# Jumping knowledge layers of a graph kernel: four blocks become one, with messages turned before they are weighed

## The chip, the core and the metric

The kernel runs on one core of a Trainium2 chip, as one launch. The metric is the device time of that launch in microseconds. Engines are called by the profile's names: PE is TensorE, DVE VectorE, ACT ScalarE, POOL GpSimd, SP SyncE. Each has its own stream of instructions, and they meet only through semaphores.

## What is computed

Four graph networks run one after the other over 50000 nodes of 128 features and 25000 edges (src, dst), sorted by dst; each adds its result to its input and normalizes the rows. The change is in the third, a stack of four layers whose outputs are combined by a maximum ("jumping knowledge"):

```python
norm_src = rsqrt(max(deg_out, 1))[:, None]
norm_dst = rsqrt(max(deg_in, 1))[:, None]
h = x
xs = []
for i in range(4):
    m = h * norm_src
    agg = segment_sum(m[src], dst, num_segments=n)
    h = agg * norm_dst
    h = relu(h @ Ws[i] + bs[i])
    mu, var = mean(h, axis=0), var(h, axis=0)          # over all nodes
    h = (h - mu) * rsqrt(var + 1e-5) * gammas[i] + betas[i]
    h = relu(h)
    xs.append(h)
out = relu(max(stack(xs), axis=0) @ lin1_w + lin1_b)
```

## The kernel before

The kernel works on edges in **slots**: 49 groups (`EG`) of 512 slots (`GROUP`), four columns (`SUB`) of 128. The sum of a node's messages stands in the slot of its last edge. Nodes without an edge all have the same row in these layers; it stands once, in row `SLOTS` of a table.

The program is a chain of blocks. A block has one stream for each engine and ends with a barrier of all of them. `run_groups(eng, n, stages)` writes an engine's stream as a software pipeline: in step k it emits, in the order of the list, each stage for group k minus its lag. Order within an engine is therefore fixed: an instruction that waits holds up all behind it. `g.lag(2)` is the group two earlier, whose buffer is used again.

`jk_start_block` makes the edge weights `l2_weight` (one number a slot, slots along the partitions) and the rows `SLOTS` of the tables `jk0` to `jk2`. Then `jk_layer_block` runs once for each layer i. For each group:

- POOL (`pool_fetch`, L570) issues four indirect DMAs that gather 128 rows each of the last layer's table into one of five message buffers. It waits until the buffer is used up.
- In layers 1 to 3 DVE (`adjust`, L1908, L1910) applies the last layer's batch norm to the rows: times a row of scales, plus a row of shifts. These rows were made at the last layer's end by `spread_column` and two products with ones on PE.
- ACT (`scalar_weigh`, L1023) scales each of the four columns by its edge weight, with the ReLU.
- PE (`tensor_sum`, L1057) transposes the four columns, so that slots lie along the free dimension.
- DVE (`vector_carry`, L1079) scans along the slots: running sums that start again with each node.
- PE (`make`, L696) multiplies by the layer's weights; ACT (`keep`, L1886) adds the bias, with ReLU.
- SP stores this tile `h_t` into `jk_t` (for the maximum at the end). Except in the last layer, PE turns it back (`turn`, L687), ACT copies the rows out of PSUM (`out`, L1891), and SP stores them into `jk{i}`, from which the next layer gathers.
- DVE (`count`, L1916, L1919) adds up values and squares for the batch norm, over last slots only.

After group 48, DVE and ACT compute mean, variance, scale and shift (L1926 to L1938), and the rows are spread. Only then does the block end, and POOL begins the next layer's gathers.

Of the kernel before, what the change touches and what calls it, by code (L numbers as in the profile page):

```python
# [299 lines left out]
class Weights:  # L300
    def __init__(self, nc, ctx):
# [15 lines left out]
        self.jk_scale_row, self.jk_shift_row = sb("jk_scale_row", [P, D]), sb("jk_shift_row", [P, D])  # L317
# [1459 lines left out]
def spread_column(dve, pe_ready, diag, ident, column):  # L1777

    dve.tensor_scalar(diag[:], ident[:], column, None, ALU.mult).then_inc(pe_ready, 1)


def jk_start_block(nc, K, W, tables):


    ph = Phase(nc, "jk_start", 0)
    row, row_ps = ph.sb("row", [LAYERS, D]), ph.ps("row_ps", [LAYERS, D])
    made, turned, copied, stored = (ph.sem(n) for n in ("made", "turned", "copied", "stored"))
    chain, to_root, root = ph.sem("chain"), ph.sem("to_root"), ph.sem("root")
    block = ph.block()

    @block.scalar
    def _(act):
        act.wait_ge(to_root, 1)
        act.activation(K.l2_weight[:], K.l2_weight[:], ACT.Sqrt).then_inc(root, 1)

    @block.vector
    def _(dve):
        link = linker(dve, chain)
        dve.tensor_scalar(K.l2_weight[:], K.src_count[:], 1.0, None, ALU.max).then_inc(to_root, 1)
        dve.tensor_scalar(W.jk_const[:], W.jk_b[:], 0.0, None, ALU.max).then_inc(made, 1)  # L1800
# [12 lines left out]
    def _(sp):
        sp.wait_ge(copied, 1)
        for i in range(LAYERS - 1):
            sp.dma_start(tables[f"jk{i}"][SLOTS:SLOTS + 1], row[i:i + 1, :]).then_inc(stored, 16)
        sp.wait_ge(stored, 16 * (LAYERS - 1))
    ph.close()


def jk_layer_block(nc, i, K, W, tables):


    ph = Phase(nc, f"jk_layer{i}", EG)
    S, A_ = ph.count_sem, ph.dma_sems
    last = i == LAYERS - 1
    sums = SegmentSums(ph, K, tables["x2"] if i == 0 else tables[f"jk{i - 1}"], K.idx if i == 0 else K.idx_jk, D, [K.l2_weight])
    h_t, h = ph.sb("h_t", [P, 2, 1, GROUP]), ph.sb("h", [P, 2, SUB, D])
    off, square = ph.sb("off", [P, GROUP]), ph.sb("square", [P, GROUP])
    off_sum, square_sum = ph.sb("off_sum", [P, EG]), ph.sb("square_sum", [P, EG])  # L1830
    small, diag = ph.sb("small", [P, 4]), [ph.sb(f"diag{b}", [P, P]) for b in range(2)]
    h_ps, rows_ps = ([ph.ps(f"{k}{b}", [P, 1, GROUP]) for b in range(2)] for k in ("h_ps", "rows_ps"))
    made, kept, turned, out_done, offset, counted = (S(n) for n in ("made", "kept", "turned", "out_done", "offset", "counted"))
    scaled, shifted = (S(n) for n in ("scaled", "shifted"))
    if i:
        ready = ph.sb("ready", [P, 2, SUB, D])
        sums.rows, sums.messages, sums.used, sums.func = ready, shifted, scaled, ACT.Relu
# [5 lines left out]
    def _(sp):  # L1843
# [9 lines left out]
        if not last:  # L1853
            wait_for_all(sp, h_stored)
# [710 lines left out]
```

## Time and profile before

| what | us |
|---|---|
| median of three runs | 6712.33 |
| lowest and highest run | 6707.89, 6729.76 |
| span of the profiled execution | 7555.6 |
| the profiled execution's own time, beside its span | not recorded |
| the blocks of the change, 4000 to 5295 us of the span | 1295.00 |

The profiled execution is one execution under the hardware profiler, and it is longer than every timed run; its span is from its first to its last instruction. Times of single instructions come from it. The end of a matmul is modelled by the profiler and not recorded, and some matmul records can be missing. What the profile names as the releaser of a wait is inferred from semaphores; semaphores are used again by later blocks, so that a name such as `sage_nodes_x_in` can stand for a semaphore that by then counts something else.

### The profile page before, as it was taken

To read this page: it belongs to the slowest core of one execution; us is meant where nothing else is said; L and a number is where in the kernel's file an instruction comes from. 1 tells how busy PE (TensorE), PEld (TensorE's weight loads), DVE (VectorE), ACT (ScalarE), POOL (GpSimd) and SP (SyncE) were. 2 spreads that over 40 slices of the span, in tenths; PEclk is the share of its full clock that TensorE was granted. 3 is DMA by queue.
4 is the path that set the end of the run, shared out by engine and by line. 5 is a ranking of instruction groups with operands and counts; after the bars stand their busy time and mean duration, and the time that the engine had idled before them with its cause. 6 is when DMAs were issued, how large, how long until landed. Compare 5 with 4: busy or idle time off the path is not lost. (4 is left out here: it accounts for less than half of the span.)

```text
span 7555.6 us, 86623 instructions
## 1 busy us (share of the span) xinstructions
PE 4855.1 (64%) x23532; PEld 3254.8 (43%) x23532; DVE 4654.8 (62%) x13695; ACT 3050.2 (40%) x6979; POOL 3999.0 (53%) x3991
## 2 busy tenths in 40 slices
PE   6888888779978625686233443434899995579211
PEld 4666665445558403575222222211555553346111
DVE  4777666223358627668674455656899995644444
ACT  3555554443334103344343333333677773245000
POOL 4565553544435466556555565656333334654766
PEclk9999999889989755796555666766899997789555
DMA  6988665776768423696343475754677675565232
GB/s 143 226 240 231 209 206 188 215 215 226 243 201 245 121 45 92 187 257 185 109 122 103 124 118 110 128 96 88 234 248 256 244 251 156 173 183 177 84 88 73
DMA packets 1104141, 1292.14 MB, mean 171 GB/s; under 512 B 133903, under 2 KB 815679, under 8 KB 1097390
## 3 DMA queue, kind: packets, MB, share of 16 engines
q1 hardware_dynamic: 973518, 1032.63, 43.5%
q0 software_dynamic: 130144, 253.97, 16.5%
q8 instruction: 197, 3.23, 0.2%
q14 instruction: 282, 2.31, 0.1%
HBM read 607.93 MB, written 682.10 MB: 171 GB/s over the span
## 5 line engine op out<-in xcount | busy, mean ns | idle before, releaser
L570 POOL DMA_INDIRECT jk_layer_msg<-jk,idx_jk x588 | 593.7, 1010 | 376.5 <-issue 173.4
L1057 PE MATMUL jk_layer_sum_ps<-ident,jk_layer_weighted 128*128 128x128 f32 x784 | 178.9, 369 | 733.6 <-ACT jk_layer_weighted L1023 382.1
L2084 POOL TENSOR_TENSOR rows_moved<-rows_x_in,w_lonely_row 128x512 f32<-128x512 f32 x98 | 124.6, 1272 | 677.3 <-DVE rows_x L671 640.9
L1057 PEld LDWEIGHTS jk_layer_sum_ps<-ident,jk_layer_weighted 128*128 128x128 f32 x784 | 114.6, 183 | 844.8 <-ACT jk_layer_weighted L1023 431.5
L1079 DVE TENSOR_TENSOR_SCAN jk_layer_sum_t<-goes_on,jk_layer_sum_t,jk_layer_sum_ps 128x512 f32<-128x512 uint8 x196 | 250.1, 1276 | 346.3 <-DMA sage_nodes_x_in<-in_x 288.0
L1886 ACT ACTIVATE jk_layer_h_t<-jk_layer_h_ps,w_jk_b 128x512 f32<-128x512 f32 x196 | 134.7, 687 | 631.8 <-DMA gat_own<-yv 337.9
L696 PE MATMUL sage_nodes_h_ps<-sage_nodes_h_t,w_ws 128*128 128x512 f32 x784 | 353.6, 594 | 0.0
L1198 DVE COPY sage_h<-sage_turn 128x512 f32<-128x512 f32 x98 | 67.8, 692 | 456.7 <-PE sage_turn L687 348.3
L894 ACT ACTIVATE sage_nodes_h_t<-sage_nodes_h_ps,w_b_c 128x512 f32<-128x512 f32 x392 | 248.9, 688 | 239.8 <-PE sage_nodes_h_ps L696 114.8
L696 PE MATMUL sage_h_ps<-sage_sum_t,w_wn 128*128 128x512 f32 x588 | 296.7, 614 | 59.0 <-issue 58.8
L2283 PE MATMUL gcn_end_sum_ps<-ident,gcn_end_rows 128*128 128x128 f32 x196 | 54.7, 434 | 426.9 <-DVE gcn_end_rows L2276 215.4
L570 POOL DMA_INDIRECT sage_msg<-h,idx x196 | 185.7, 948 | 247.4 <-ACT sage_weighted L1023 166.4
L570 POOL DMA_INDIRECT sage_end_msg<-h,idx x196 | 193.8, 989 | 224.4 <-ACT sage_end_weighted L1023 113.5
L696 PE MATMUL jk_layer_h_ps<-jk_layer_sum_t,w_jk_w 128*128 128x512 f32 x392 | 297.0, 852 | 0.6 <-DVE jk_layer_sum_t L1079 0.4
L687 PE MATMUL sage_nodes_ring<-ident,sage_nodes_h_t 128*128 128x128 f32 x1568 | 221.9, 288 | 106.7 <-issue 98.7
L696 PE MATMUL sage_h_ps<-sage_own_t,w_ws 128*128 128x512 f32 x588 | 290.0, 602 | 0.0
L1627 POOL DMA_INDIRECT second_msg<-u,idx_y x196 | 185.4, 946 | 182.4 <-PE second_x_ps L679 108.3
L1137 POOL DMA_INDIRECT place_of_src<-place,src_node x196 | 185.5, 947 | 167.7 <-issue 67.6
L1179 ACT ACTIVATE sage_h_t<-sage_h_ps,w_b_c 128x512 f32<-128x512 f32 x196 | 124.3, 685 | 357.9 <-PE sage_h_ps L696 296.6
L570 POOL DMA_INDIRECT jk_layer_msg<-x,idx x196 | 194.4, 992 | 139.2 <-issue 57.7
L570 POOL DMA_INDIRECT gcn_msg<-r,idx x196 | 191.9, 979 | 142.4 <-DVE gcn_rows L2276 65.8
L557 POOL DMA_INDIRECT src_count<-counts,src_node x196 | 192.3, 981 | 138.3 <-SPq L135 93.6
(454 smaller groups left out, 16299.8 us busy)
## 6 DMA issues: line engine op xcount, KB each, us to landing
h<-sage_nodes_h SPq DMA_DIRECT2D x196, 512.0 KB
h_t<-sage_h_t SPq DMA_DIRECT2D x98, 512.0 KB
h<-sage_h SPq DMA_DIRECT2D x98, 512.0 KB
jk_t<-jk_layer_h_t SPq DMA_DIRECT2D x196, 256.0 KB
rows_layers<-jk_t SPq DMA_DIRECT2D x49, 1024.0 KB, 5.9
r<-rows_h SPq DMA_DIRECT2D x98, 512.0 KB
second_x_in<-u SPq DMA_DIRECT2D x147, 260.0 KB
jk<-jk_layer_h SPq DMA_DIRECT2D x147, 256.0 KB
```

Of the source, the lines that this page charges most:

```text
L557: pool.indirect_dma_start(out=self.K.src_count[:, t:t + 1], out_offset=None, in_=self.table, in_offset=bass.IndirectOffsetOnAxis(ap=self.K ...
L570: pool.indirect_dma_start(out=into[:, g.number % depth, s, :], out_offset=None, in_=table, in_offset=bass.IndirectOffsetOnAxis(ap=index_ti ...
L687: mm = pe.transpose(ps[:, n, c * P:(c + 1) * P], feats[:, c, s * P:(s + 1) * P], ident[:])
L696: mm = pe.matmul(ps[:, c, :], w[:, k, c * P:(c + 1) * P], x[:, k, :], start=n == 0, stop=n == len(terms) - 1)
L894: ins = act.activation(tile[:, g.b, c, :], ps[:, c, :], ACT.Relu, bias=bias[:, c:c + 1])
L1057: mm = pe.transpose(ps[:, c, at_s], self.weighted[:, g.b, s, c * P:(c + 1) * P], self.K.ident[:])
L1079: dve.tensor_tensor_scan(self.sum_t[:, g.b, c, :], self.K.goes_on[:, cols(g, GROUP)], self.ps[g.b][:, c, :], self.sum_t[:, 1 - g.b, c, GRO ...
L1137: pool.indirect_dma_start(out=K.place[:, t:t + 1], out_offset=None, in_=tables["place"], in_offset=bass.IndirectOffsetOnAxis(ap=K.src_node ...
L1179: ins = act.activation(h_t[:, g.b, c, :], h_ps[:, c, :], ACT.Relu, bias=bias[:, c:c + 1])
L1627: pool.indirect_dma_start(out=msg[:, r % 4, s, :], out_offset=None, in_=tables["u"], in_offset=bass.IndirectOffsetOnAxis(ap=K.idx_y[:, col ...
L1886: act.activation(h_t[:, g.b, 0, :], h_ps[g.b][:, 0, :], ACT.Relu, bias=W.jk_b[:, i:i + 1]).then_inc(kept.sem, 1)
L2084: pool.tensor_tensor(moved[:, g.b], x_in[:, g.number % 3], to_subs(W.lonely_row), ALU.add).then_inc(lonely_added.sem, 1)
```

## The change

`jk_start_block` and the four `jk_layer_block` become one `jk_block`. Groups are counted on through all layers (`job(i, g)`), with one barrier at the end. In detail:

- POOL's message ring is 8 deep; its first gather of layer i waits only for the last three stores of the rows of layer i-1, and no longer for that layer's statistics.
- PE transposes the raw messages (`turn_messages`). In layers 1 to 3 ACT then applies the last batch norm and ReLU on the transposed tile (`norm`), where scale and shift are one number a partition. The rows of scales and shifts and their spreading go.
- The edge weights are turned once, stored in DRAM as `l2_row`, and for each group of each layer SP loads the 512 weights into all 128 partitions (`load_weight`). DVE multiplies (`weigh`), out of PSUM in layer 0, out of SBUF in the others. ACT's four scalings go.
- The scan's input is now a tile in SBUF, `product`. `sum_t`, `h_t` and `h` have three buffers instead of two.
- PE's stages are `turn_messages` at lag 0, `make` at 2 and `turn` at 3, where they were 0, 1 and 2.

```diff
-    sums = SegmentSums(ph, K, tables["x2"] if i == 0 else tables[f"jk{i - 1}"], ..., D, [K.l2_weight])
+    deep = 8
+    msg = ph.sb("msg", [P, deep, SUB, D])
+    weight = ph.sb("weight", [P, 3, GROUP])
...
     @block.sync
+        sp.wait_ge(l2_copied, 1)
+        sp.dma_start(tables["l2_row"].rearrange("(h q p) -> q h p", h=2, p=P), l2_rows[:]).then_inc(l2_stored, 16)
+        sp.wait_ge(l2_stored, 16)
+        for i in layers:
+            def load_weight(g):
+                j = job(i, g)
+                wait_for(sp, weighed, j.lag(3))
+                sp.dma_start(weight[:, j.number % 3, :], tables["l2_row"][cols(g, GROUP)].partition_broadcast(P)).then_inc(weight_in.of(j), 16)
...
+            run_groups(sp, EG, [(load_weight, -2), (store_t, 2)] + ([] if i == LAST else [(store, 3)]))
     @block.gpsimd
+            if i:
+                for k in range(3):
+                    wait_for(pool, h_stored, Group(i * EG - 1 - k))
...
     @block.tensor
+            def turn_messages(g):
+                j = job(i, g)
+                wait_for(pe, arrived, j)
...
+                turn_rows(pe, msg_ps[j.b][:, 0, :], msg[:, j.number % deep], K.ident).then_inc(msg_turned.sem, 1)
...
+            run_groups(pe, EG, [(turn_messages, 0), (make, 2)] + ([] if i == LAST else [(turn, 3)]))
     @block.scalar
+            def norm(g):
+                j = job(i, g)
+                wait_for(act, msg_turned, j)
+                wait_for(act, weighed, j.lag(2))
+                act.activation(ready[:, j.b], msg_ps[j.b][:, 0, :], ACT.Relu, bias=W.jk_shift[:, i - 1:i], scale=W.jk_scale[:, i - 1:i]).then_inc(normed.sem, 1)
...
+            run_groups(act, EG, ([(norm, 0)] if i else []) + [(keep, 2)] + ([] if i == LAST else [(out, 3)]))
     @block.vector
-            dve.tensor_tensor(m, sums.msg[:, g.number % sums.depth], to_subs(W.jk_scale_row), ALU.mult).then_inc(scaled.sem, 1)
-            dve.tensor_tensor(m, m, to_subs(W.jk_shift_row), ALU.add).then_inc(shifted.sem, 1)
+                dve.tensor_tensor(product[:, j.b], rows, weight[:, j.number % 3], ALU.mult).then_inc(weighed.sem, 1)
...
+                dve.tensor_tensor_scan(sum_t[:, j.number % 3, 0, :], K.goes_on[:, cols(g, GROUP)], product[:, j.b], ...)
+            run_groups(dve, EG, [(carry, 1), (weigh, 0), (count, 3)])
```

On ACT, the border between layer 0 and layer 1 stood as follows; `jk_layer_small` is the column of statistics, the two L135/L1878 rows are the block's end and the next one's beginning:

```order
L1886 ACTIVATE jk_layer_h_t<-jk_layer_h_ps,w_jk_b 128x512
L1891 COPY jk_layer_h<-jk_layer_rows_ps 128x512 x2
L1897 ACTIVATE jk_layer_small<-jk_layer_small,w_eps 128x1
L135 UNCONDITIONAL_BRANCH
L1878 UNCONDITIONAL_BRANCH
L1023 ACTIVATE jk_layer_weighted<-jk_layer_ready,l_weight 128x128 x8
L1886 ACTIVATE jk_layer_h_t<-jk_layer_h_ps,w_jk_b 128x512
L1023 ACTIVATE jk_layer_weighted<-jk_layer_ready,l_weight 128x128 x4
L1886 ACTIVATE jk_layer_h_t<-jk_layer_h_ps,w_jk_b 128x512
```

Now the same place reads as follows (`jk_ready` is the tile after the batch norm):

```order
L1905 ACTIVATE jk_h_t<-jk_h_ps,w_jk_b 128x512
L1911 COPY jk_h<-jk_rows_ps 128x512 x2
L1916 ACTIVATE jk_small<-jk_small,w_eps 128x1
L1896 ACTIVATE jk_ready<-jk_msg_ps,w_jk_shift,w_jk_scale 128x512 x3
L1905 ACTIVATE jk_h_t<-jk_h_ps,w_jk_b 128x512
L1896 ACTIVATE jk_ready<-jk_msg_ps,w_jk_shift,w_jk_scale 128x512
L1905 ACTIVATE jk_h_t<-jk_h_ps,w_jk_b 128x512
L1911 COPY jk_h<-jk_rows_ps 128x512
L1896 ACTIVATE jk_ready<-jk_msg_ps,w_jk_shift,w_jk_scale 128x512
L1905 ACTIVATE jk_h_t<-jk_h_ps,w_jk_b 128x512
L1911 COPY jk_h<-jk_rows_ps 128x512
```

The block's end has gone, and three norms of layer 1 come before its first `keep`, where eight scalings did.

On DVE, one group in the middle of layer 1 was `count`, `adjust` and the scan:

```order
L1910 TENSOR_TENSOR jk_layer_ready<-jk_layer_ready,w_jk_shift_row 128x512
L1079 SCALAR_TENSOR_TENSOR jk_layer_sum_t<-goes_on,jk_layer_sum_t,jk_layer_sum_ps 128x512
L1916 SCALAR_TENSOR_TENSOR jk_layer_off,jk_layer_off_sum<-jk_layer_h_t,w_jk_const,last_row 128x512
L1919 SCALAR_TENSOR_TENSOR jk_layer_square,jk_layer_square_sum<-jk_layer_off 128x512
L1908 TENSOR_TENSOR jk_layer_ready<-jk_layer_msg,w_jk_scale_row 128x512
```

Now it is one product in place of the two operations of `adjust`, with its input from ACT and the weights from SP:

```order
L1963 SCALAR_TENSOR_TENSOR jk_square,jk_square_sum<-jk_off 128x512
L1952 SCALAR_TENSOR_TENSOR jk_sum_t<-goes_on,jk_sum_t,jk_product 128x512
L1941 TENSOR_TENSOR jk_product<-jk_ready,jk_weight 128x512
L1960 SCALAR_TENSOR_TENSOR jk_off,jk_off_sum<-jk_h_t,w_jk_const,last_row 128x512
L1963 SCALAR_TENSOR_TENSOR jk_square,jk_square_sum<-jk_off 128x512
```

On SP, the start of layer 0 had only the tables' rows and stores:

```order
L1816 DMA jk<-jk_start_row 1x128 x3
L135 UNCONDITIONAL_BRANCH
L1842 UNCONDITIONAL_BRANCH
L1846 DMA jk_t<-jk_layer_h_t 128x512 x2
L1850 DMA jk<-jk_layer_h 128x4x128
L1846 DMA jk_t<-jk_layer_h_t 128x512
L1850 DMA jk<-jk_layer_h 128x4x128
L1846 DMA jk_t<-jk_layer_h_t 128x512
```

Now the weights' row is stored first, and each step begins with a load:

```order
L1817 DMA jk<-jk_const_row 1x128 x3
L1819 DMA l_row<-jk_l_rows 98x2x128
L1825 DMA jk_weight<-l_row 128x512 x5
L1830 DMA jk_t<-jk_h_t 128x512
L1825 DMA jk_weight<-l_row 128x512
L1830 DMA jk_t<-jk_h_t 128x512
L1835 DMA jk<-jk_h 128x4x128
L1825 DMA jk_weight<-l_row 128x512
L1830 DMA jk_t<-jk_h_t 128x512
L1835 DMA jk<-jk_h 128x4x128
L1825 DMA jk_weight<-l_row 128x512
```

The loads of weights stand ahead of the stores in SP's queue, five of them before the first store.

## Rows read from the trace of the kernel before

**Rows 1.** Head of the page.

```profile
span 7555.6 us, 86623 instructions
```

**Rows 2.** Windows of layers 0 to 3: their sum; us busy by engine.

```profile
sum 1295.00, PE 537.90 PEld 299.71 DVE 725.62 ACT 441.89 POOL 788.10; mean PE 134.47 PEld 74.93 DVE 181.40 ACT 110.47 POOL 197.03
```

**Rows 3.** Groups by line, POOL, layer 0, then layer 1: busy, mean ns | idle, releasers.

```profile
L570 POOL DMA_INDIRECT jk_layer_msg<-x,idx x196 | 194.4, 992 | 139.2 <-issue 57.7 <-POOLq L137 40.9 <-ACT jk_layer_weighted L1023 40.5
...
L570 POOL DMA_INDIRECT jk_layer_msg<-jk,idx_jk x196 | 197.5, 1007 | 129.1 <-issue 57.3 <-DVE jk_layer_ready L1908 42.6 <-POOLq L137 29.1
```

**Rows 4.** Timeline, end of layer 0: start, us, engine, line, names [idle before].

```profile
4302.04 1.11 PE L1057 MATMUL jk_layer_sum_ps<-ident,jk_layer_weighted 128*128 128x128 f32 x4 [3.44 <-ACT jk_layer_weighted L1023]
...
4302.95 1.91 PE L696 MATMUL jk_layer_h_ps<-jk_layer_sum_t,w_jk_w 128*128 128x512 f32 x2
...
4304.90 0.69 ACT L1886 ACTIVATE jk_layer_h_t<-jk_layer_h_ps,w_jk_b 128x512 f32<-128x512 f32 x1 [2.44 <-PE jk_layer_h_ps L696]
...
4309.66 0.69 ACT L1886 ACTIVATE jk_layer_h_t<-jk_layer_h_ps,w_jk_b 128x512 f32<-128x512 f32 x1 [2.45 <-PE jk_layer_h_ps L696]
...
4313.12 0.69 ACT L1886 ACTIVATE jk_layer_h_t<-jk_layer_h_ps,w_jk_b 128x512 f32<-128x512 f32 x1 [1.14 <-PE jk_layer_h_ps L696]
```

**Rows 5.** Timeline, layer 0, near its start.

```profile
4028.35 0.66 PE L1057 MATMUL jk_layer_sum_ps<-ident,jk_layer_weighted 128*128 128x128 f32 x4 [1.44 <-issue]
...
4035.99 1.28 DVE L1079 TENSOR_TENSOR_SCAN jk_layer_sum_t<-goes_on,jk_layer_sum_t,jk_layer_sum_ps 128x512 f32<-128x512 uint8 x1 [7.66 <-DMA sage_nodes_x_in<-in_x]
...
4040.19 0.69 ACT L1886 ACTIVATE jk_layer_h_t<-jk_layer_h_ps,w_jk_b 128x512 f32<-128x512 f32 x1 [11.43 <-DMA gat_own<-yv]
```

**Rows 6.** Waits in the block of last rows: in total, times, longest.

```profile
ACT rows_y L2171 <- PE rows_bank_y L705: 7.8, 11, 0.7
```

**Rows 7.** Groups by line, POOL, the whole kernel.

```profile
L570 POOL DMA_INDIRECT jk_layer_msg<-jk,idx_jk x588 | 593.7, 1010 | 376.5 <-issue 173.4 <-DVE jk_layer_ready L1908 114.5 <-POOLq L137 88.6
...
L1627 POOL DMA_INDIRECT second_msg<-u,idx_y x196 | 185.4, 946 | 182.4 <-PE second_x_ps L679 108.3 <-issue 46.3 <-POOLq L137 24.7
```

**Rows 8.** Groups by line and shape, layer 1.

```profile
L1079 DVE TENSOR_TENSOR_SCAN jk_layer_sum_t<-goes_on,jk_layer_sum_t,jk_layer_sum_ps 128x512 f32<-128x512 uint8 x49 | 62.5, 1275 | 80.9 <-DMA sage_nodes_x_in<-in_x 70.9 <-DMA gat_own<-yv 10.0
L1023 ACT ACTIVATE jk_layer_weighted<-jk_layer_ready,l_weight 128x128 f32<-128x128 f32 x196 | 62.2, 389 | 22.4 <-DVE jk_layer_ready L1910 14.7 <-issue 7.7
...
L1916 DVE SCALAR_TENSOR_TENSOR jk_layer_off<-jk_layer_h_t,w_jk_const,last_row 128x512 f32<-128x512 f32 x49 | 36.4, 744 | 25.1 <-ACT jk_layer_h_t L1886 13.0 <-issue 12.1
...
L1908 DVE TENSOR_TENSOR jk_layer_ready<-jk_layer_msg,w_jk_scale_row 128x512 f32<-128x512 f32 x49 | 33.6, 686 | 17.2 <-DMA jk_layer_msg<-jk,idx_jk 17.1
```

**Rows 9.** Timeline: start of layer 0, then the border to layer 1.

```profile
4001.19 0.26 DVE L1799 TENSOR_SCALAR l_weight<-src_count 128x196 f32<-128x196 f32 x1 [3.45 <-PEq L137]
...
4005.52 0.95 POOL L570 DMA_INDIRECT jk_layer_msg<-x,idx  x1 [40.89 <-POOLq L137]
...
4009.27 0.95 POOL L570 DMA_INDIRECT jk_layer_msg<-x,idx  x1 [0.31 <-issue]
...
4011.74 1.28 ACT L1023 ACTIVATE jk_layer_weighted<-jk_layer_msg,l_weight 128x128 f32<-128x128 f32 x4 [9.89 <-DMA jk_layer_msg<-x,idx]
...
4297.27 0.95 POOL L570 DMA_INDIRECT jk_layer_msg<-x,idx  x1 [0.30 <-issue]
...
4320.47 0.20 DVE L1926 TENSOR_REDUCE jk_layer_small<-jk_layer_off_sum 128x1 f32<-128x49 f32 x1
...
4327.35 0.95 POOL L570 DMA_INDIRECT jk_layer_msg<-jk,idx_jk  x1 [29.12 <-POOLq L137]
```

**Rows 10.** DMA queues in 280 us of layer 1, then 270 us of layer 3.

```profile
q0 software_dynamic: 5810, 11.91, 47.3%
q1 hardware_dynamic: 26901, 21.18, 22.6%
...
q0 software_dynamic: 5820, 11.94, 38.3%
q1 hardware_dynamic: 5765, 10.50, 10.3%
```

More of the change, by code:

```diff
@@ L1791, in _, with keep, out @@
     @block.scalar
     def _(act):
-        act.wait_ge(to_root, 1)
-        act.activation(K.l2_weight[:], K.l2_weight[:], ACT.Sqrt).then_inc(root, 1)
+        act.wait_ge(l2_capped, 1)
+        act.activation(K.l2_weight[:], K.l2_weight[:], ACT.Sqrt).then_inc(l2_root, 1)
+        for i in layers:
+            def norm(g):
+                j = job(i, g)
+                wait_for(act, msg_turned, j)
+                wait_for(act, weighed, j.lag(2))
+                act.activation(ready[:, j.b], msg_ps[j.b][:, 0, :], ACT.Relu, bias=W.jk_shift[:, i - 1:i], scale=W.jk_scale[:, i - 1:i]).then_inc(normed.sem, 1)
+            def keep(g):
+                j = job(i, g)
+                wait_for(act, made, j)
+                wait_for(act, ht_stored, j.lag(3))
+                wait_for(act, counted, j.lag(3))
+                if i < LAST:
+                    wait_for(act, turned, j.lag(3))
+                act.activation(h_t[:, j.number % 3, 0, :], h_ps[j.b][:, 0, :], ACT.Relu, bias=W.jk_b[:, i:i + 1]).then_inc(kept.sem, 1)
+            def out(g):
+                j = job(i, g)
+                wait_for(act, turned, j)
+                wait_for(act, h_stored, j.lag(3))
+                act.copy(h[:, j.number % 3], lanes(rows_ps[j.b][:, 0, :], D)).then_inc(out_done.sem, 1)
+            if i:
+                act.wait_ge(scale_ready, i)
+            run_groups(act, EG, ([(norm, 0)] if i else []) + [(keep, 2)] + ([] if i == LAST else [(out, 3)]))
+            act.wait_ge(to_root, i + 1)
+            act.activation(small[:, 3:4], small[:, 1:2], ACT.Sqrt, bias=W.eps[:]).then_inc(rooted, 1)
@@ new lines, in _ @@
+        dve.tensor_scalar(K.l2_weight[:], K.src_count[:], 1.0, None, ALU.max).then_inc(l2_capped, 1)
+        dve.tensor_scalar(W.jk_const[:], W.jk_b[:], 0.0, None, ALU.max).then_inc(const_made, 1)
+        dve.wait_ge(const_turned, 1)
+        dve.tensor_copy(const_row[:], const_ps[:]).then_inc(const_copied, 1)
+        dve.wait_ge(l2_root, 1)
+        link(dve.reciprocal(K.l2_weight[:], K.l2_weight[:]))
+        dve.tensor_tensor(K.l2_weight[:], K.l2_weight[:], K.norm_dst[:], ALU.mult).then_inc(l2_ready, 1)
@@ L2528, in resnorm_gnn @@
         mean_block(nc, A, K, W, tables)
-        jk_start_block(nc, K, W, tables)
-        for i in range(LAYERS):
-            jk_layer_block(nc, i, K, W, tables)
+        jk_block(nc, K, W, tables)
         ends.close()
```

259 lines of the change are left out of this document (126 added, 133 removed).

## The prediction

> **What bounds the kernel now.** I read the page first [rows 1]: the profiled execution spans 7555.6 us, and it is 843 us longer than the median of the three timed runs, 6712.33 us (span over median 1.126). No other time of that execution is given. So whatever the trace shows must be read with the question which part of it the profiled execution alone has. The windows by stage come second: the five blocks that the change touches, from 4000 to 5295 us, take 1295 us of the span in four nearly equal layers [rows 2].
>
> Third, the groups by line on POOL. In each layer POOL issues 196 gathers; one takes 0.99 to 1.01 us and is followed by 0.30 us of issue [rows 3]. Four gathers make a group: 49 x 4 x 1.29 = 252 us a layer, 1008 of the 1295 us. The rest of layers 0 and 1 on POOL is a wait for ScalarE or VectorE to free one of the five message buffers (40.5 and 42.6 us) and the wait at the border between blocks (40.9 and 29.1 us).
>
> Why does POOL ever wait for a buffer? The timeline says that the engines behind it can go faster: with the slow TensorE clock (a product of 1.91 us) ScalarE's `keep` comes after 4.76 us, with the fast one after 3.46 us [rows 4], against 5.15 us for four gathers. But now and then TensorE's results come late. Its four transposes are shown to end at 4029.01, yet the scan that needs them starts at 4035.99, with VectorE idle for 7.66 us, and `keep` waits 11.43 us, to 4040.19 [rows 5]; nothing that VectorE or ScalarE wait for there is a DMA, whatever the inferred releaser says. These delays return with about every fifth group. In the block of last rows, where no gather runs, nothing like it exists: the longest wait of ScalarE for TensorE's `bank_y` is 0.7 us [rows 6].
>
> So the main question is whether the timed runs have these delays. POOL's waits for another engine in just three of its sixteen groups of indirect DMAs, 114.5 and 40.5 us here and 108.3 in the block `second`, are already 263 us [rows 3, 7], and such waits are the only large idle that could go away between profiled and timed execution, since one gather needs its 1.25 us either way. I take it as likelier that most of the 843 us are these delays, and that the timed kernel is bound by POOL in these layers: 4 x 252 + borders, some 1075 us.
>
> **The change, part by part.** *Weighing.* ScalarE loses four scalings of 389 ns a group and, in layers 1 to 3, gains one norm of a 128x512 tile out of PSUM, like `keep`'s 0.69 us: 1.56 becomes 0.69 us. VectorE loses the multiply by the row of scales and the add of the row of shifts (686 ns, and the add alike) and gains one product of the same size; in layer 0 it only gains the product [rows 4, 8]. PE's work is the same: four transposes, one product, four turns. All of it lies beside POOL's 5.15 us a group, so it is worth nothing there; without POOL as cover it would be the 4.76 us step that shrinks, at most by 0.7 us x 196 = 137 us.
>
> *Eight buffers instead of five, three instead of two behind.* Worth what POOL waits for buffers: nothing if the timed runs have no delays, 40.5 + 114.5 = 155 us if they have all of them [rows 3, 7].
>
> *Borders.* Before, the last gather of layer 0 starts at 4297.27 and the first of layer 1 at 4327.35; of this, 6.88 us are statistics, spreading of the rows and the barrier, from 4320.47 [rows 9]. Without late results I build the same border from rows: 2.47 us from the last gather's start to the scaling that needs it (4009.27 to 4011.74), scaling 1.28, on PE sum, product, turn, product 1.11 + 1.91 + 1.06 (four transposes, like the sum) + 1.91 [rows 4], `keep` 0.69, `count` 1.7 (two passes like the 744 ns one [rows 8] with their small reads), then 6.88: 19.0 us. After, POOL no longer waits for statistics, only for the stored rows: 2.47, but PE now has three products and four turns left behind the last transposes, 1.1 + 5.7 + 4.2 = 11.0, copy 0.57, store about 2.5 (as a gather): 16.6 us. With the fast clock, PE parts nearly halved, it is 16.2 against 11.7. Between 2.4 and 4.5 us, so 3.4 x 3 = 10 us gained. The start: POOL's first gather is at 4005.52 and could follow the barrier at about 4001.7, as VectorE does at 4001.19 [rows 9]: 4 us gained. The row of weights must be turned, stored and loaded first, two DMA trips of 2.5 us behind 4004; the first product is then ready near 4010, about when the first messages are.
>
> *Port between VectorE and POOL.* A gather takes 946 ns on average in the block `second`, 992 in layer 0 and 1007 in layer 1 [rows 3, 7]. What goes up with it is VectorE's work with two SBUF inputs: two operations of about 0.7 us in layer 0, four in layer 1 [rows 8]. If a gather that meets one waits for its end, the cost grows with the sum of squared lengths: 0.5 gives 46 ns, 1.0 gives 61 ns. After, the scan (1275 ns) has its data in SBUF and no longer in PSUM. If it counts like the others the sum is 1.3 to 1.6, some 85 to 95 ns: 35 ns x 784 = 27 us lost. If it doesn't count, layers 1 to 3 have three operations instead of four: 8 us gained. I take 10 us lost. The Trainium skill (SBUF — State Buffer, "Who interferes with whom") says that a VectorE instruction with two SBUF inputs contends with a GpSimd instruction that reads SBUF; by that the scan counts and the loss would be the 27 us. The same section infers that a tensor_tensor doesn't touch descriptor writing; the rise from 946 to 1007 ns doesn't bear that out.
>
> *DMA.* 196 loads of 256 KB are new. In 280 us of layer 1, 11.91 MB of gathers (45.4 groups) took 47.3% of the sixteen engines and 21.18 MB of stores 22.6%: 2.92 + 1.57 = 4.5 us a group. In layer 3, with half the stores, gathers took 2.27 us a group and the stores 10.3% of 270 us for 10.50 MB, 2.65 us a MB [rows 10]. A load is 0.26 MB, 0.7 us a group: 5.2 us in layers 1 and 2, as much as POOL's 5.15; 3.6 to 4.1 in the others. I take nothing for it, with 8 buffers as cover; the dear end is under the rivals.
>
> The sum: -10 - 4 + 10 + 0 = -4 us, to 6708 us.
>
> **The rivals.** *The delays are real.* For it: the trace has them, and the other 843 us may be in DMAs or issue. Against it: that POOL's idle would then leave no room for the 843 us. Then 155 us of POOL's buffer waits go, and 14 us at borders: 6543 us. Eight buffers hold 41 us of gathers, more than the longest delay here. If half is real: 6630 us.
>
> *DMA becomes the bound in layers 1 and 2* (the other side). For it: gathers there cost 0.65 us a group more than in layer 3, where one 256 KB stream less runs beside them; another stream may cost as much again. Then 5.2 + 0.65 = 5.85 us a group, 0.7 over POOL: 49 x 2 x 0.7 = 69 us lost; with 0.3 it is 34. It decides from the point where the DMA engines need over 5.15 us a group. Against it: part of a packet's time is waiting and not work. With the scan at the port (27 us) and 14 us gained at borders this gives 6712 + 34 to 69 + 13 = 6760 to 6795 us.
>
> *The scan alone takes the port:* 6712 - 14 + 27 = 6725 us, still no change that can be told.
>
> **How the numbers follow.** About 0.3%, 20 us, is what a measurement of this kernel can tell. Forecast (6692 to 6732 us, the port case within it): 0.33. Delays real, wholly 0.2 or partly 0.2: faster, 0.40. DMA bound, or DMA and port: slower, 0.27. The predicted time is the single likeliest case's, 6708. The range goes from 6540, which leaves out little under the full gain, to 6770, which takes in the lower price of the DMA case; both bounds of port and borders lie inside. Likeliest case alone: 6690 to 6735.
>
> **What would show it.** POOL's gaps for buffers gone in the changed trace, with a time that stays, would show that the timed runs never had them; a time 100 us or more lower, that they had. Mean of a gather near 1.03 us: the scan takes the port; near 0.99: it doesn't. Packets of layers 1 and 2 at over 0.9 share of the DMA engines, and POOL, TensorE waiting for messages: DMA bound. The border between layers should fall from 30 us to 12 to 17. I am wrong above all if one gather is cheaper in timed runs than 1.25 us, since then the engines behind POOL set the pace and what they lose in work counts.

## The result and the profile after

| | us, median (lowest to highest) | runs |
|---|---|---|
| before | 6718.84 (6707.89 to 6729.76) | 4 |
| changed | 6787.66 (6778.96 to 6807.84) | 4 |

The ratio is 1.0108, 95% interval 1.0093 to 1.0123: 69 us slower. I had forecast 6708 us, no change.

The changed kernel's profiled execution lasted as long as its timed runs, 6786.5 us, so its trace can be read as it stands. The trace behind the prediction could not be, so I profiled the kernel before once more (first experiment below, 6721.6 us); the comparison here is with that. First the groups of gathers on POOL, of the changed kernel (layers 1 to 3, then layer 0), which answer to [rows 3, 7]:

```profile
L1853 POOL DMA_INDIRECT jk_msg<-jk,idx_jk x588 | 628.7, 1069 | 276.1 <-issue 174.6 <-DMA jk<-jk_h 90.8 <-PE jk_msg_ps L679 10.6
L1853 POOL DMA_INDIRECT jk_msg<-x,idx x196 | 217.5, 1110 | 80.2 <-issue 57.3 <-POOLq L137 20.8 <-PE jk_msg_ps L679 2.1
```

and the same of the kernel before, profiled again:

```profile
L570 POOL DMA_INDIRECT jk_layer_msg<-jk,idx_jk x588 | 593.3, 1009 | 257.9 <-issue 174.6 <-POOLq L137 71.1 <-DVE jk_layer_ready L1908 12.2
...
L570 POOL DMA_INDIRECT jk_layer_msg<-x,idx x196 | 196.3, 1002 | 85.2 <-issue 59.4 <-POOLq L137 25.8
```

A gather went from 1009 to 1069 ns in layers 1 to 3 and from 1002 to 1110 ns in layer 0: 588 x 60 + 196 x 108 ns = 56 us more. Waits for buffers are small in both (10.6 and 2.1 us against 12.2). The wait for the last layer's rows or the barrier, 90.8 us for three borders, was 71.1 us.

Now one window for each layer with the border behind it; a row ends with the granted clock, the busy share of the DMA engines, and GB/s. The changed kernel:

```profile
core 0: us, PE busy (x) PEld busy (x) DVE busy (x) ACT busy (x) POOL busy (x), PEclk, DMA share, GB/s
3460.00:3745.00 285.00, 141.12 (x480) 88.64 (x481) 158.29 (x290) 56.76 (x94) 217.51 (x196) 0.72 0.62 175
3745.00:4045.00 300.00, 137.95 (x467) 81.02 (x466) 149.03 (x284) 91.83 (x140) 208.03 (x196) 0.67 0.92 166
4045.00:4350.00 305.00, 146.38 (x489) 86.78 (x486) 158.77 (x302) 95.89 (x147) 208.48 (x196) 0.70 0.90 166
4350.00:4660.00 310.00, 137.29 (x338) 61.56 (x336) 182.39 (x357) 81.25 (x116) 212.21 (x196) 0.63 0.68 138
```

and the kernel before, profiled again:

```profile
3465.00:3738.00 273.00, 148.09 (x487) 85.52 (x487) 135.88 (x250) 118.41 (x294) 196.34 (x196) 0.70 0.54 140
3738.00:4023.00 285.00, 147.96 (x481) 87.20 (x482) 193.59 (x353) 117.10 (x292) 198.49 (x196) 0.68 0.87 133
4023.00:4311.00 288.00, 148.33 (x493) 85.65 (x491) 194.72 (x355) 118.09 (x294) 197.61 (x196) 0.69 0.87 134
4311.00:4597.00 286.00, 124.31 (x318) 54.84 (x318) 202.81 (x383) 98.61 (x254) 197.16 (x196) 0.67 0.55 96
```

In both kernels the DMA engines are busy 0.87 to 0.92 of the time in layers 1 and 2, and much less in layers 0 and 3 (0.54 to 0.68). The kernel before was thus at the edge already. In the first profile layer 1 read 47.3% and 22.6%, 0.70 together [rows 10]: its pace was slower, and a group's gathers took less of the DMA engines there (2.92 us, against 3.59 in run 1).

Last the border between layers 1 and 2 of the changed kernel, POOL's last gather of one layer and first of the next, with VectorE's scans between them:

```profile
4025.82 0.95 POOL L1853 DMA_INDIRECT jk_msg<-jk,idx_jk  x1 [0.31 <-issue]
4062.64 0.94 POOL L1853 DMA_INDIRECT jk_msg<-jk,idx_jk  x1 [35.87 <-DMA jk<-jk_h]
```

```profile
4036.18 1.28 DVE L1952 TENSOR_TENSOR_SCAN jk_sum_t<-goes_on,jk_sum_t,jk_product 128x512 f32<-128x512 uint8 x1
...
4039.36 1.28 DVE L1952 TENSOR_TENSOR_SCAN jk_sum_t<-goes_on,jk_sum_t,jk_product 128x512 f32<-128x512 uint8 x1
```

POOL has issued everything at 4027 and then waits 35.87 us. Ten scans follow each other at 3.18 us from 4026.62 to 4055.28: VectorE, no longer held up by anything, works off the groups that are left. What held it up before shows in the waits from 3912 to 4026 (in total, times, longest):

```profile
DVE jk_product L1941 <- DMA jk_weight<-l_row: 68.9, 13, 8.4
ACT jk_h L1911 <- DMA jk<-jk_h: 49.5, 13, 7.3
...
PE jk_msg_ps L679 <- DMA jk_msg<-jk,idx_jk: 8.6, 4, 3.7
```

VectorE waits for weights and ScalarE for the end of a store, so that its buffer can be used again. TensorE waits little for messages here and from 3952 on not at all; earlier in the layer it did (91.5 us from 3752 to 3912). So when the DMA engines fall behind, what is late at the end of a layer are the loads and stores on SP's queue. A ring of eight message buffers hides this from POOL, but the groups that are not worked off when the last gather is issued are paid for at the border. The same border of the kernel before, profiled again, was shorter:

```profile
4037.03 0.94 POOL L570 DMA_INDIRECT jk_layer_msg<-jk,idx_jk  x1 [28.18 <-POOLq L137]
```

From the first gather's start and the last one's end in each layer, on POOL's timeline, I made this ledger (us; "end" is from the last gather to the next block's first instruction):

| kernel | layers 0 / 1 / 2 / 3 | borders | end | in all |
|---|---|---|---|---|
| before, profiled again | 255.8 / 262.1 / 261.4 / 256.6 | 17.5 / 28.2 / 25.4 | 16.2 | 1123.2 |
| changed | 276.9 / 274.4 / 267.9 / 271.6 | 14.8 / 35.9 / 40.2 | 17.1 | 1198.8 |

The block is 75.6 us longer: 54.9 in the layers, 19.8 in the borders, 0.9 at the end. It starts 5 us earlier (the wait in front of its first gather is 20.8 us, was 25.8), which leaves 71 us of the 69 measured.

### The profile page after: what moved, and what is told of

Read it like the earlier page. It is cut to its first block and busy times, and to the rows that moved or that the text cites. A ratio compares the mean times of both kernels' runs of the same rounds, so it can differ in the third digit from the quotient of the medians.

```text
span 6786.5 us, 85990 instructions
## 1 busy us (share of the span) xinstructions
PE 4757.1 (70%) x23518; PEld 3216.2 (47%) x23522; DVE 4564.9 (67%) x13586; ACT 2932.8 (43%) x6342; POOL 4063.1 (60%) x3991
## 5 line engine op out<-in xcount | busy, mean ns | idle before, releaser
L1853 POOL DMA_INDIRECT jk_msg<-jk,idx_jk x588 | 628.7, 1069 | 276.1 <-issue 174.6
L679 PE MATMUL jk_msg_ps<-ident,jk_msg 128*128 128x128 f32 x784 | 187.3, 384 | 501.9 <-DMA jk_msg<-jk,idx_jk 360.5
L679 PEld LDWEIGHTS jk_msg_ps<-ident,jk_msg 128*128 128x128 f32 x784 | 127.9, 195 | 604.2 <-DMA jk_msg<-jk,idx_jk 452.2
L696 PE MATMUL jk_h_ps<-jk_sum_t,w_jk_w 128*128 128x512 f32 x392 | 319.6, 912 | 124.3 <-DVE jk_sum_t L1952 124.3
L1905 ACT ACTIVATE jk_h_t<-jk_h_ps,w_jk_b 128x512 f32<-128x512 f32 x196 | 134.7, 687 | 381.9 <-PE jk_h_ps L696 327.2
L1853 POOL DMA_INDIRECT jk_msg<-x,idx x196 | 217.5, 1110 | 80.2 <-issue 57.3
L599 POOL DMA_INDIRECT kept<-u,idx x196 | 194.9, 994 | 113.1 <-issue 59.4
L570 POOL DMA_INDIRECT sage_nodes_fetched<-in_x,src_x x196 | 205.4, 1048 | 95.1 <-issue 49.1
L671 DVE TENSOR_SCALAR rows_z<-rows_y,rows_norm_moments,rows_norm_root 128x128 f32<-128x128 f32 x392 | 255.5, 711 | 3.6
L570 POOL DMA_INDIRECT gcn_end_msg<-y,idx x196 | 188.6, 962 | 108.3 <-issue 59.4
```

The lines of the kernel that those rows point to most:

```text
L570: pool.indirect_dma_start(out=into[:, g.number % depth, s, :], out_offset=None, in_=table, in_offset=bass.IndirectOffsetOnAxis(ap=index_ti ...
L599: pool.indirect_dma_start(out=kept[:, t, :], out_offset=None, in_=table, in_offset=bass.IndirectOffsetOnAxis(ap=K.idx[:, t:t + 1], axis=0) ...
L671: ins = dve.tensor_scalar(out[:, g.number % depth, s, :], rows[:, g.b, s, :], self.moments[:, g.b, s, 0:1], self.root[:, g.b, s, 0:1], ALU ...
L679: mm = pe.transpose(ps[:, s * P:(s + 1) * P], rows[:, s, :], ident[:])
L696: mm = pe.matmul(ps[:, c, :], w[:, k, c * P:(c + 1) * P], x[:, k, :], start=n == 0, stop=n == len(terms) - 1)
L1853: pool.indirect_dma_start(out=msg[:, j.number % deep, s, :], out_offset=None, in_=table, in_offset=bass.IndirectOffsetOnAxis(ap=index[:, g ...
```

## The experiments

Two theories. **Port:** the scan's data now come from SBUF, a gather that meets the scan waits, and POOL's pace falls. **DMA:** the loads of weights overload the DMA engines, transfers come late, and borders pay. Ratios are to the kernel before on the same chip. Ledgers are made as the one above.

### 1. The kernel before, profiled again

No edit.

> The kernel before, profiled a second time. If the late TensorE results belonged only to the first profiled execution, the span is 6700 to 6740 us, ScalarE's longest wait for TensorE in the four layers is under 4 us, the layers take 1125 to 1140 us in all (1200 us of the changed kernel less the 70 us by which it is slower), and POOL waits for buffers under 15 us. If they are real, the span is over 7000 us and POOL's waits for buffers are again some 150 us.

It took 6723.41 us with a span of 6721.6. These are its waits of ScalarE's `keep` for TensorE, and of POOL for a buffer, in the four layers (in total, times, longest):

```profile
ACT jk_layer_h_t L1886 <- PE jk_layer_h_ps L696: 333.5, 161, 2.9
...
POOL jk_layer_msg L570 <- DVE jk_layer_ready L1908: 12.2, 12, 3.8
```

The longest is 2.9 us where the first profile had 11.43 [rows 5]; POOL's waits for buffers are 12.2 us where it had 155 [rows 3, 7]. This execution took as long as the timed runs (6707.89 to 6729.76 us), so the late TensorE results are not in them.

### 2. Weights loaded for three groups only

```diff
-                wait_for(sp, weighed, j.lag(3))
-                sp.dma_start(weight[:, j.number % 3, :], ...)
+                if j.number < 3:
+                    sp.dma_start(weight[:, j.number % 3, :], ...)
...
-                wait_for(dve, weight_in, j)
+                if j.number < 3:
+                    wait_for(dve, weight_in, j)
```

All later groups are weighed with the weights of the first three, so this kernel leaves out part of the computation.

> The changed kernel, but weights are loaded for the first three groups only and used for all groups (the other groups' weights are left out of the computation). Theory DMA (the 193 other loads make messages late, and the backlog of up to eight groups is paid at the borders): the borders between layers fall from 36 and 40 us to 12 to 17, a gather falls to about 1.0 us, and the time is 6700 to 6725 us. Theory port (the scan's SBUF input lengthens the gathers): a gather stays at 1.07 to 1.11 us and only the borders' part is gained, 6740 to 6760 us.

6745.57 us, ratio 1.0036 (1.0022 to 1.0050): 42 us of the loss are gone. Theory DMA alone had expected 6700 to 6725 us, theory port alone 6740 to 6760.

```profile
L1853 POOL DMA_INDIRECT jk_msg<-jk,idx_jk x588 | 631.0, 1073 | 226.2 <-issue 176.4 <-DMA jk<-jk_h 48.0 <-PE jk_msg_ps L679 1.8
```

The borders are 15.3 / 17.7 / 15.0 us, 43 less than in the changed kernel, and the gathers stayed long, at 1073 and, in layer 0, 1094 ns. So the loads cost at the borders and not through the gather's length. Each theory had half of it right: the borders fell as DMA said, the gathers stayed long as port said. There are two causes.

### 3. Product in PSUM

```diff
-                dve.tensor_tensor(product[:, j.b], rows, weight[:, j.number % 3], ALU.mult).then_inc(weighed.sem, 1)
+                dve.tensor_tensor(product[j.b][:], rows, weight[:, j.number % 3], ALU.mult).then_inc(weighed.sem, 1)
...
-                dve.tensor_tensor_scan(sum_t[:, j.number % 3, 0, :], K.goes_on[:, cols(g, GROUP)], product[:, j.b],
+                dve.tensor_tensor_scan(sum_t[:, j.number % 3, 0, :], K.goes_on[:, cols(g, GROUP)], product[j.b][:],
```

Here `product` is two PSUM tiles.

> The changed kernel with the product written to PSUM, so that the scan reads its data from PSUM as before. Theory port: the mean gather falls by 0.06 to 0.1 us to about 1.0 us, which is 784 x 0.075 = 59 us, 6725 to 6740 us. Theory DMA: no change, 6780 to 6795 us, gathers within 0.02 us of 1.07 and 1.11.

6768.21 us, 1.0076 (1.0059 to 1.0093). Layers 1 to 3, layer 0, then the window of layer 1:

```profile
L1854 POOL DMA_INDIRECT jk_msg<-jk,idx_jk x588 | 585.7, 996 | 310.0 <-issue 171.9 <-DMA jk<-jk_h 96.8 <-PE jk_msg_ps L679 41.4
...
L1854 POOL DMA_INDIRECT jk_msg<-x,idx x196 | 194.7, 993 | 80.2 <-issue 57.6 <-POOLq L137 20.8 <-PE jk_msg_ps L679 1.8
```

```profile
3740.00:4010.00 270.00, 117.48 (x395) 69.21 (x396) 122.61 (x223) 74.86 (x114) 194.08 (x196) 0.68 0.94 154
```

The mean gather falls to 996 and 993 ns, 66 us in all. The edit moves the product's write as well as the scan's input, but the timelines tell the two apart: 93 gathers start in the first 1.1 us of a scan here, and none takes over 0.95 us; in the changed kernel 104 of 106 such gathers took over 1 us. So the length is the scan's: shown. But only 20 us arrive in the time. POOL now waits 41.4 us for buffers and 96.8 us at the borders (16.2 / 46.6 / 33.9), and VectorE 208.5 us for weights where it had waited 154.0, with the DMA engines busy 0.94 of layer 1. What the port gives back, the DMA engines take. Neither theory had this number.

### 4. Five buffers instead of eight

```diff
-    deep = 8
+    deep = 5
```

> The changed kernel with five message buffers in place of eight. If messages are late because the DMA engines lack time, depth only shifts where it is paid: POOL waits for buffers, the borders fall to some 25 us, and the time stays within 10 us of 6788. If the depth itself does harm, since loads of weights stand behind eight groups of gathers in the DMA engines' rings, the time falls by 20 to 60 us, and VectorE's wait for weights (154 us) at least halves.

6783.21 us, 1.0095 (1.0078 to 1.0112), which can't be told from the changed kernel. The later borders are 24.5 and 29.5 us instead of 35.9 and 40.2, and the layers 8.2 us longer. VectorE waits 144 us for weights (154 in the changed kernel), so the depth isn't what delays them. Depth shifts the bill and hardly changes it.

### 5. The constant row 128 times

Of the 25000 edges, 16290 come from a node that has no incoming edge. All of these messages are read from one row, `SLOTS`, in layers 1 to 3. Here each partition has its own copy:

```diff
-        dve.tensor_scalar(K.idx_jk[:], where[:], float(SLOTS), None, ALU.min)
+        link(dve.tensor_copy(first_copy[:], K.slot_no[:, 0:1]))        # partition number
+        link(dve.tensor_scalar(first_copy[:], first_copy[:], float(SLOTS), None, ALU.add))
+        dve.tensor_scalar(K.idx_jk[:], where[:], first_copy[:], None, ALU.min)
...
-            sp.dma_start(tables[f"jk{i}"][SLOTS:SLOTS + 1], const_row[i:i + 1, :]).then_inc(const_stored, 16)
+            sp.dma_start(tables[f"jk{i}"][SLOTS:SLOTS + P], const_row[:, i, :]).then_inc(const_stored, 16)
```

> The changed kernel, but the constant row of the nodes without an edge stands 128 times at the end of each table, and each partition gathers its own copy. Theory hot row (the gathers' packets of layers 1 to 3 are slow because 65% of them read one and the same row): the mean packet of a gather falls from 0.6 to 0.85 us to layer 0's 0.28 us, the borders of layers 1 to 2 and 2 to 3 fall from 36 and 40 us to 15 to 18, the mean gather on POOL stays at 1.06 to 1.11 us, and the time is near that of the kernel with weights loaded once, 6735 to 6755 us. Rival (packets are slow because of the loads and stores beside them): borders and time stay, 6775 to 6795 us.

6750.62 us, 1.0040 (1.0025 to 1.0054). DMA queues in 260 us of layer 1 (packets, MB, share of 16 engines), changed kernel, then this one:

```profile
q0 software_dynamic: 5898, 12.09, 60.3%
q1 hardware_dynamic: 29750, 29.05, 34.5%
```

```profile
q1 hardware_dynamic: 35520, 34.61, 41.1%
q0 software_dynamic: 5837, 11.94, 20.0%
```

The same 12 MB of gathers take 20.0% instead of 60.3%, as in layer 0 of the changed kernel (20.4%); the borders are 15.9 / 15.0 / 14.4 us, and the gather on POOL stays long (1092 ns). All the loads of weights are still there. So at this kernel's pace it takes both, a hot row (one that most gathers read) and the loads, to make transfers late; taking away either gives back some 40 us.

### 6. Runs 2 and 3 together

The two edits above in one kernel.

> The changed kernel with both: weights loaded for the first three groups only (the others' weights are left out of the computation), and the product in PSUM. If port and DMA are the two causes and add up: gathers at 0.99 us, layers of 254 to 257 us, borders of 15 to 18 us, in all 1085 us from the first gather to the end of the block, 38 us under the kernel before: 6675 to 6700 us. If a third thing holds the layers, over 6710 us.

6717.05 us, 0.9993 (0.9982 to 1.0005), higher than the 6675 to 6700 expected. Gathers are 1011 and 991 ns, the layers 253.7 to 259.7, but the borders 12.7 / 32.1 / 22.4 us, where run 2 had 15.3 / 17.7 / 15.0 at the slower pace. At POOL's faster pace the hot row alone makes transfers late, as in the kernel before.

### 7. Weights spread by TensorE

```diff
+            def spread_weight(g):
+                wait_for(pe, weighed, j.lag(2))
+                for s in range(SUB):
+                    mm = pe.matmul(weight_ps[j.b][:, s * P:(s + 1) * P],
+                                   K.l2_weight[:, g.number * SUB + s:g.number * SUB + s + 1].broadcast_to([P, P]), K.ident[:], start=True, stop=True)
+                mm.then_inc(spread.sem, 1)
...
-                dve.tensor_tensor(product[:, j.b], rows, weight[:, j.number % 3], ALU.mult).then_inc(weighed.sem, 1)
+                dve.tensor_tensor(msg_ps[j.b][:, 0, :], rows, weight_ps[j.b][:], ALU.mult).then_inc(weighed.sem, 1)
```

`rows` is ScalarE's tile in layer 0 too; the scan reads `msg_ps`; the loads of weights go.

> The changed kernel, but TensorE spreads the weights: four products of a column of weights (the same for all output partitions) with the identity write 128x512 weights to PSUM; ScalarE copies the messages in layer 0 as it norms them in the others, and VectorE's product goes back to PSUM. No load of weights, no SBUF input of the scan's data. Both causes are then gone at a price of 1.2 to 1.8 us of TensorE a group: 6675 to 6700 us if TensorE stays under POOL's 5.1 us a group. If TensorE (now 4.1 to 4.7 us a group, at the slow clock) becomes the bound, the layers take over 262 us each and the time is over 6710 us.

6725.13 us, 0.9995 (0.9985 to 1.0005), again higher than the 6675 to 6700 expected. Layers 253.9 to 259.8, borders 15.8 / 30.0 / 43.8. TensorE isn't the bound (VectorE waits for its weights 4.5 us in the whole block); the hot row is, as run 9 shows, which differs by the copies alone.

### 8. The kernel before with 128 copies

The edit of run 5, in `jk_start_block`.

> The kernel before with the constant row 128 times in each table. Theory hot row: its borders of layers 1 to 2 and 2 to 3, 28 and 25 us, fall to the 17.5 us of the border behind layer 0, and POOL's waits for buffers (12 us) go: 6690 to 6708 us. Rival: no change, 6712 to 6728 us.

6703.78 us, 0.9970 (0.9958 to 0.9981): 22 us faster than the kernel before. Queues in 245 us of layer 1, first the kernel before as profiled again, then with copies:

```profile
q0 software_dynamic: 5733, 11.76, 65.7%
q1 hardware_dynamic: 27590, 21.73, 26.3%
```

```profile
q1 hardware_dynamic: 29371, 23.17, 28.8%
q0 software_dynamic: 5888, 12.07, 24.7%
```

Borders are 19.3 / 19.7 / 18.7 us. One group of gathers took 0.657 x 245 us / (11.76 MB / 0.262 MB a group) = 3.59 us of the sixteen engines and now takes 1.31. Without `jk` stores beside them, in layer 3 of run 1, gathers of the same hot row took 0.458 x 230 us / (11.50 MB / 0.262 MB) = 2.40 us: what runs beside them counts too.

### 9. Weights from TensorE, 128 copies

> Weights spread by TensorE and product in PSUM, as in the run with these two alone, and the constant row in 128 copies. If the port and the hot row are all that holds the block, the layers take 254 to 257 us and all three borders 14 to 16: 1081 us from the first gather to the end, 42 us under the kernel before, 6675 to 6695 us. If TensorE's extra products have a price of their own, borders over 18 us or POOL waits for buffers, 6700 us or more.

6671.47 us, 0.9918 (0.9904 to 0.9931), 54 us under the kernel before on the same chip and a little under the 6675 expected: both causes gone.

```profile
L1847 POOL DMA_INDIRECT jk_msg<-jk,idx_jk x588 | 580.8, 988 | 219.0 <-issue 178.0 <-DMA jk<-jk_h 40.7 <-PE jk_msg_ps L681 0.3
...
L1847 POOL DMA_INDIRECT jk_msg<-x,idx x196 | 191.3, 976 | 80.2 <-issue 59.4 <-POOLq L137 20.8
```

```profile
3745.00:3985.00 240.00, 162.82 (x820) 123.24 (x820) 147.45 (x268) 89.70 (x136) 183.43 (x185) 0.83 0.54 149
```

Gathers at 988 and 976 ns, layers 250.7 to 253.3, borders 13.8 / 12.9 / 14.0, in all 1065.1 us.

### 10. Product in PSUM, 128 copies, weights still loaded

> The changed kernel with the product in PSUM and the constant row in 128 copies; SP still loads the 196 rows of weights into all partitions. If loads cost only through the lateness that the hot row makes, the time equals that with weights from TensorE, 6675 to 6695 us. If 256 KB more a group cost by themselves (0.7 us a group of the DMA engines), borders or waits for weights grow and it is 6700 to 6725 us.

6677.90 us, 0.9926 (0.9912 to 0.9940). Queues in 240 us of layer 1:

```profile
q1 hardware_dynamic: 35605, 34.74, 44.3%
q0 software_dynamic: 5815, 11.93, 22.7%
```

Layers 252.8 to 257.9, borders 14.6 / 14.0 / 13.9, in all 1080.0 us. With the hot row gone, the loads delay next to nothing: both queues together are at 0.67, and VectorE waits for weights once, 5.4 us, where the changed kernel has (in total, times, longest)

```profile
DVE jk_product L1941 <- DMA jk_weight<-l_row: 154.0, 34, 8.4
```

Against run 9 the trace shows 15 us more, 13 of it in gathers of 1006 and 987 ns. These are the product's: its two inputs are both in SBUF in layers 1 to 3 here, and the gathers that start within it together take 13 us more than at 0.94 us each; in run 9, where the weights are in PSUM, such gathers take 0.94. The times, 6 us apart, don't tell the two kernels apart.

### 11. Squares on ScalarE

Run 9, with `square` moved (at lag 4, with two buffers of `off`):

```diff
-                dve.scalar_tensor_tensor(square[:], off[:], 1.0, off[:], ALU.mult, ALU.mult,
-                                         accum_out=square_sum[:, cols(g, 1)]).then_inc(counted.sem, 1)
+                act.activation(square[:], off[:, j.b], ACT.Square, accum_out=square_sum[:, cols(g, 1)]).then_inc(counted.sem, 1)
```

> As the kernel with weights from TensorE and 128 copies, and the squares of the statistics move from VectorE to ScalarE (Square with a running sum), so that VectorE has one operation on two SBUF inputs a group, count's first, besides a product and a scan with one each. Theory port: the mean gather falls from 0.99 to 0.96 or 0.97 us, 784 x 0.025 = 20 us, 6655 to 6675 us. Rival (an operation that reads one tile twice doesn't count): the time stays within 6 us of the kernel without this move.

6656.81 us, 0.9895 (0.9880 to 0.9910), the fastest, 69 us under the kernel before on the same chip.

```profile
L1847 POOL DMA_INDIRECT jk_msg<-jk,idx_jk x588 | 572.8, 974 | 220.9 <-issue 178.3 <-DMA jk<-jk_h 42.6
```

The gather falls by 14 ns in layers 1 to 3 and not at all in layer 0 (976 ns both times): 8 us, less than half of what theory port expected. Means of gathers differ by up to 28 ns between two profiles of one kernel (layer 2 in the first profile of the changed kernel and in run 12), so these 14 ns are not shown to come from the move. The rival's premise is refuted all the same: in run 9, 63 of the 69 gathers that start within `square`, which reads one tile twice, take over 1 us. The median fell by 15 us against run 9; from where is open.

### 12. The changed kernel again

> The changed kernel again, on the chip of the other three, so that each of their differences has both ends on one chip: 1.009 to 1.012 of the kernel before, borders of 15, 36 and 40 us and gathers at 1.06 to 1.11 us as in its first profile.

6789.59 us, 1.0089 (1.0074 to 1.0105), gathers of 1089 and 1095 ns, borders 16.0 / 28.2 / 38.1. The result holds in a second measurement. It also shows how finely one trace can be read: the layers are 11 us longer than in the first profile, the borders 8 us shorter, the middle one 28.2 us where 36 were expected; and the ratio is 1.0089 where it was 1.0108, which is 13 us. The single terms below are good to some 10 us.

## Why the prediction was wrong

Its own sum, term by term; the whole is 71 us by the ledger and the start, where -4 stood:

| term | forecast | measured |
|---|---|---|
| start | -4 | -5 |
| port (all of the layers' growth) | +10, range -8 to +27 | +55 |
| DMA, the loads' lateness | 0, rival 34 to 69 | +43 (run 2 against the changed kernel) |
| borders otherwise | -10 | -23 (71.1 to run 2's 48.0) |
| weighing, eight buffers | 0 | nothing seen; block's end +1 |

**Reading the first profile: right.** Run 1 shows that the late TensorE results aren't in the timed runs. The rival that they are real, to which I gave 0.40 of the chances, falls. The sign that I had named came too: POOL's waits for buffers went away in the changed trace, and the time stayed (it even rose).

**Port: right in kind, wrong in size.** This is the step that failed most: the sum had 10 us, its dear end 27, and it is 55. The rule of the Trainium skill (SBUF — State Buffer, "Who interferes with whom"), that VectorE with two SBUF inputs contends with a GpSimd instruction that reads SBUF, is borne out for the scan by run 3: 1069 to 996 ns when one input moves to PSUM. What I had wrong is the price of a meeting, which I took from squared lengths, scaled by the 46 and 61 ns that short operations had cost. Timeline of layer 0 of the changed kernel, VectorE's scans and POOL's gathers:

```profile
3585.28 1.28 DVE L1952 TENSOR_TENSOR_SCAN jk_sum_t<-goes_on,jk_sum_t,jk_product 128x512 f32<-128x512 uint8 x1
...
3585.75 1.57 POOL L1853 DMA_INDIRECT jk_msg<-x,idx  x1 [0.30 <-issue]
...
3588.70 1.28 DVE L1952 TENSOR_TENSOR_SCAN jk_sum_t<-goes_on,jk_sum_t,jk_product 128x512 f32<-128x512 uint8 x1
...
3589.15 1.58 POOL L1853 DMA_INDIRECT jk_msg<-x,idx  x1 [0.30 <-issue]
...
3591.03 0.94 POOL L1853 DMA_INDIRECT jk_msg<-x,idx  x1 [0.30 <-issue]
```

The scan runs from 3585.28 to 3586.56; the gather that starts 0.47 us into it ends at 3587.32. The next pair is the same, 3588.70 to 3589.98 and 3590.73. Both gathers end 0.75 us behind the scan (within 0.01) and take 1.57 us where a free one takes 0.94.

Counted over the four layers, 106 gathers of the changed kernel start in the first 1.1 us of a scan; 104 of them are longer than 1 us, and each of these ends 0.75 us behind its scan (0.747 to 0.757). Together they take 65 us more than at 0.94 us each. The other operations cost 8 us less than in run 1, which leaves 57 us, the 56 of the gathers' means. In run 1 as many, 113, start so, and none takes over 0.96 us. The meetings are thus not new; only their price is. A scan of 1.28 us is as long as the 1.25 us from one gather to the next, so nearly every scan catches a gather's start.

The price follows from these rows: a gather that starts s into the scan takes 1.28 + 0.75 - s, which is 1.09 - s more than 0.94. With starts spread evenly 1.25 us apart that is 1.09 x 1.09 / (2 x 1.25) = 0.48 us a scan, an estimate of 93 us for 196 scans. Squared lengths had given 27 us for the exchange, so some 35 for the scan alone, with the 8 us for the operation that went. The scan cost 65. It is under the 93, because the starts are not spread evenly: of the 174 gathers that start in a scan, 100 do so 0.4 to 0.6 us into it and 68 in its last 0.2 us, where they cost nothing. Why they settle there was only read from the timeline, not tested.

**DMA: taken as 0, and it was the rival.** This is the second step that failed. One load was priced right: 0.7 us of the sixteen engines, and run 10 shows it: q1 takes 0.443 x 240 = 106.3 us for 34.74 MB, in run 9 without loads 0.306 x 240 = 73.4 us for 23.34 MB, which is 32.9 us for 11.40 MB or 0.76 us a load. The base was wrong. I had 4.5 us a group for gathers and stores, from an execution at a slower pace, in which a group's gathers took 2.92 us; in run 1, at the timed pace, they take 3.59, the sum is 0.92 x 245 us / 44.9 groups = 5.0 us, and with a load 5.8, beyond the 5.15 from which I had let this rival decide. And I laid the dearer packets of layer 1 to the stream of stores beside them. Runs 5 and 8 show that most of it is the one row: with 128 copies a group's gathers take 1.31 us and not 3.59. The first trace could have said so. Its layer 0 has the same stores and the same number of gathers, and its DMA engines are busy 0.47 of the time against 0.70 in layer 1; the gathers in 280 us of it:

```profile
q0 software_dynamic: 5936, 12.17, 22.8%
```

That is 1.38 us a group, against 2.92 in layer 1. Eight message buffers were no cover, since the weights have three and the stores' tiles three, and since the backlog piles up over the layer and is paid at its end. The sign that I had named, TensorE waiting for messages, is not what marks it: at the end of a layer VectorE waits for weights and ScalarE for stores.

The rival "DMA, or DMA and port", at 0.27, was the right one, and its 6760 to 6795 us hold the 6787.66 measured. That its number fits so well is in part luck: it had the port at 27 us, half of what it cost, and the loads at up to 69, more than the 43 that run 2 gives back.

**Borders: the built term was right, what stands on it wasn't.** Where no transfer is late, three borders fall from 57.7 us (run 8) to 45.3 (run 5), 12 where 10 were forecast, and the first one from 17.5 to 14.8, inside the 2.4 to 4.5. The other two were forecast at 12 to 17 us and came to 35.9 and 40.2, for the lateness. The further 11 us of the -23 are the lateness that the hot row causes in the kernel before (71.1 against 57.7 us with copies) and that run 2, at POOL's slower pace, hardly has (48.0 against 45.3). Run 6 bears this out: no loads either, POOL at its faster pace, and 67.3 us of borders. That is how the two losses partly hide each other, and why run 3 gave back 20 us and not 66.

What stays open: why reading one row from many descriptors is slow, why the border behind layer 2 is longer than that behind layer 1 in some kernels and shorter in others (30.0 and 43.8 us in run 7, 32.1 and 22.4 in run 6), and where run 11 gained.

## What to carry to other kernels

Before pricing a new DMA stream, look for a stage with the same transfers at a much lower share of the DMA engines: a dear packet can be a hot row, and 128 copies of it cost nothing here and gave 22 us by themselves. A ring of buffers hides late transfers until the last gather is issued; a border that grows in the later stages is where to look for a DMA engine that falls behind. Moving an operand of VectorE's scan between PSUM and SBUF changes POOL's gathers, so an intermediate tile is better in PSUM when GpSimd issues gathers beside it. And when two resources are near their limit, expect little from mending one.

## What the runs showed of the hardware

- 65% of the gathered rows on one address (layer 1, with stores beside them): 3.59 us of the sixteen engines a group; on 128 addresses, one for each partition: 1.31 us.
- A gather that starts in the first 1.1 us of VectorE's scan on two SBUF inputs ends 0.75 us after it (104 of 106); at the usual 0.4 to 0.6 us into it this makes 1.57 instead of 0.94 us. One that starts in the scan's last 0.2 us takes 0.94 (68 of 68).
- The same holds for VectorE's product, a tensor_tensor. With both inputs in SBUF, 45 of the 64 gathers that start within it take over 1 us, up to 1.46 (layers 1 to 3 of the changed kernel); with one input in PSUM none of 16 does in layer 0, and none of 100 in run 9.
- With more products on TensorE its clock was higher. In layer 1 the granted clock is 0.71 of the full 2.4 GHz in run 10 (some of the time at 1.2 GHz) and 0.83 in run 9, where each group has four more products; the mean product of `make` took 888 ns in the one and 761 ns in the other. POOL waited 0.3 us for buffers in run 9's layers 1 to 3, so the spreading of weights cost it nothing.
- A single profiled execution can differ from all timed ones: the first profile of the kernel before was 834 us longer than the second (7555.6 and 6721.6 us), with TensorE's results up to 7 us late.
